# A four-layer graph network on one core: the gathers of layers 2 and 3 wait for two chunks at a time instead of eight

## What is computed

```python
# layer 2
K, Q, V = x_aug @ Wk, x_aug @ Wq, x_aug @ Wv            # 8 heads of 16
attn = einsum('ehd,ehd->eh', Q[dst], K[src]) * rel_scale[rel] / 4
attn_exp = exp(attn - max(attn))
out = segment_sum(attn_exp / (segment_sum(attn_exp)[dst] + 1e-16) * V[src])
# layer 3
scores = einsum('ehd,ehd->eh', q[src], k[tgt]) / 4 + edges @ We + be
scores = scores * cons[tgt] + mlp(distances)
weights = exp(scores - segment_max(scores)[tgt]) / segment_sum(...)[tgt]
agg = segment_sum(weights * v[tgt])
```

## Time and profile before

| | |
|---|---|
| median of three executions | 8839.98 us (8818.74 to 8856.99) |
| the profiled execution | 8825.96 us, its span 8824.2 us |
| busy over the span: PE, DVE, POOL, ACT | 65%, 56%, 54%, 13% |
| mean granted TensorE clock | 0.69 of full speed |
| gathers of layer 2: first, last start | 5723.2, 7302.6 us |
| gathers of layer 3: first, last start | 7425.1, 8709.4 us |

### The profile page before, as it was taken

One profiled execution on the slowest core, in us unless ns is written; L12 is line 12 of the kernel. 1 busy time (PEld: TensorE's weight loads), 2 busy tenths in 40 slices (PEclk: granted clock), 3 DMA queues, 4 the chain that ended last, 5 costly groups with the idle time before them and its releaser, 6 DMA issues. The chain is left out here.

```text
span 8824.2 us, 135351 instructions
## 1 busy us (share of the span) xinstructions
PE 5731.9 (65%) x29121; PEld 4795.7 (54%) x29122; DVE 4911.5 (56%) x17353; ACT 1162.1 (13%) x3262; POOL 4752.3 (54%) x4627
## 2 busy tenths in 40 slices
PE   6555555677767767777777999756666665333334
PEld 5555554566656656666664666456666664333333
DVE  6555554455555645555556888645555553444445
ACT  1111111111111101111112222100000002000001
POOL 2655665455555445555544777445554542666664
PEclk6555555777777878777778999866566666555556
DMA  5334334333333333333332444333333333333332
GB/s 155 95 93 96 96 94 105 116 96 93 95 94 93 75 89 97 92 96 93 97 77 45 60 63 60 84 83 89 90 91 87 90 87 52 74 75 75 75 77 48
DMA packets 919075, 759.30 MB, mean 86 GB/s; under 512 B 585447, under 2 KB 750451, under 8 KB 916947
## 3 DMA queue, kind: packets, MB, share of 16 engines
q0 software_dynamic: 233264, 421.09, 19.7%
q1 hardware_dynamic: 676780, 323.84, 15.2%
q10 hardware_dynamic: 8960, 13.52, 0.6%
HBM read 676.11 MB, written 80.55 MB: 86 GB/s over the span
## 5 line engine op out<-in xcount | busy, mean ns | idle before, releaser
L1180 POOL DMA_INDIRECT there<-table_wide,idx x1664 | 1596.4, 959 | 1382.6 <-DVE prod L1203 620.3
L1271 PE MATMUL ps<-here,hot_t 128*128 x3328 | 1228.1, 504 | 619.1 <-DVE there L1222 586.0
L2273 POOL DMA_INDIRECT there<-table_wide,idx x832 | 793.6, 954 | 888.6 <-DVE msg L2349 416.6
L1222 DVE TENSOR_TENSOR there<-there,ps 128x512 f32<-128x512 f32 x832 | 571.0, 686 | 1148.5 <-remote 579.9
L1271 PEld LDWEIGHTS ps<-here,hot_t 128*128 128x128 f32 x3328 | 735.1, 245 | 740.6 <-issue 653.8
L693 POOL DMA_INDIRECT rec<-out_recd,posd x806 | 819.1, 1016 | 568.9 <-issue 228.8
L2888 POOL DMA_INDIRECT there<-table_narrow,idx x832 | 791.2, 951 | 615.5 <-issue 252.4
L1279 PE MATMUL ps<-relu,hot_s 128*128 128x128 f32 x3328 | 885.5, 359 | 137.6 <-DVE hot_s L1211 111.1
L3048 PE MATMUL ps<-here,hot_t 128*128 x1664 | 426.5, 432 | 813.5 <-DVE prod L2969 403.1
L1279 PEld LDWEIGHTS ps<-relu,hot_s 128*128 128x128 f32 x3328 | 689.9, 239 | 328.3 <-issue 274.8
L3048 PEld LDWEIGHTS ps<-here,hot_t 128*128 128x128 f32 x1664 | 363.7, 312 | 876.0 <-issue 875.4
(11 more groups left out here) (508 smaller groups left out, 9850.2 us busy)
## 6 DMA issues: line engine op xcount, KB each, us to landing
locrows<-loc_row SPq DMA_DIRECT2D x416, 256.0 KB
krowd<-key_row SPq DMA_DIRECT2D x201, 256.0 KB
there<-table_wide,idx POOLq DMA_INDIRECT x2496
src_rows1a<-slot_src_row SPq DMA_DIRECT2D x52, 512.0 KB
lrowd<-lo_row SPq DMA_DIRECT2D x201, 128.0 KB
attr_raw<-in_edge_attr SPq DMA_DIRECT2D x201, 128.0 KB
there<-table_narrow,idx POOLq DMA_INDIRECT x832
rec<-out_recd,posd POOLq DMA_INDIRECT x806
```

What stands on the lines that cost most here:

```text
L1180: nc.gpsimd.indirect_dma_start(there[:, j, q, :], None, table, bass.IndirectOffsetOnAxis(idx[:, j, q:q + 1], 0)).then_inc(gathered[j][q], 16)
L1222: nc.vector.tensor_tensor(pair, pair, ps[:, WORK, :], ALU.add).then_inc(summed, 1)
L1271: last = nc.tensor.matmul(ps[:, WORK, (q % 2) * 2 * F:(q % 2 + 1) * 2 * F], hot_t[:, j % 2, q * P:(q + 1) * P], here[:, :, :].rearrange("p ...
L2273: nc.gpsimd.indirect_dma_start(there[:, j, q, :], None, table, bass.IndirectOffsetOnAxis(idx[:, j, q:q + 1], 0)).then_inc(gathered[j][q], 16)
```

## The change

POOL waits before every second gather, for the piece that frees the two chunks it is about to overwrite, instead of once before all eight for all four pieces; `admitted` is counted up four times as often. Nothing else changes.

```diff
 # hgt_pass, layer 2
                 for j in range(RING):
                     pool.wait_ge(indexed[j], i * 16 + 16)
-                    pool.wait_ge(placed, i * (RING * PIECES) + ((j + 1) * PIECES))
-                    pool.sem_inc(admitted, 1)
                     for q in range(U):
+                        if q % PIECE == 0:
+                            pool.wait_ge(placed, i * (RING * PIECES) + (j * PIECES + q // PIECE + 1))
+                            pool.sem_inc(admitted, 1)
                         nc.gpsimd.indirect_dma_start(there[:, j, q, :], None, table, ...)
 # edge_scores, layer 3
                 for j in range(RING):
                     pool.wait_ge(indexed, i * RING + (j + 1))
-                    pool.wait_ge(multiplied, i * (RING * PR) + (j * PR + PR))
-                    pool.sem_inc(admitted, 1)
                     for q in range(U):
+                        if q % 2 == 0:
+                            pool.wait_ge(multiplied, i * (RING * PR) + (j * PR + q // 2 + 1))
+                            pool.sem_inc(admitted, 1)
                         nc.gpsimd.indirect_dma_start(there[:, j, q, :], None, table, ...)
```

## The result

The changed kernel took 8869.2 us (median of 20 executions), the kernel before on the same chip 8827.4 us: a ratio of 1.0047 (1.0032 to 1.0062). A second comparison gave 1.0041 (1.0019 to 1.0063). So the change costs about 40 us, where a gain of 99 us had been forecast; 8869.2 us lies outside the stated range of 8690 to 8860. The profiled execution took 8864.5 us, its span is 8862.8 us.

What follows compares the result with a forecast made beforehand. No engine was full; layer 2's loop from `msg` through gather batch and first product bound it, 15.13 us a group. 98 x 1.01 = 99 us off the 8840 us median gave 8741, predicted 8742, range 8690 to 8860.

Steps and rivals of the forecast that it cites:

- The batch's start: Layer 2: the first gather waits for the first `msg`, not the fourth, so the batch begins 1.01 us earlier, still 0.78 us behind.
- What 1.01 us is worth: Layer 2's loop: the batch's progress lets the product go, so each round shortens by 1.01 us; 98 x 1.01 = 99 us.
- no change: Rival: layer 2's product release is tied to something DVE times, such as SyncE's loads; 8825 to 8840 us, chance 0.20.
- the 4.35 us: Layer 2: time from a first product to the end of the `msg` behind it, read from one round.
- The gathers as the cause: Layer 2: gathers being issued and landing hold the product; without them first products stand 7.62 us apart, half of 15.13.
- The added instructions at 0: Both layers: three more waits and three more `sem_inc` a group run while the gather before them works; cost 0.
- the 0.9 that I gave: Most the added waits and counts could cost if not covered: one more 0.30 us gap each, 0.9 us a group.
- Slower: Rival: layer 2's second product falls beside the batch and is held, 2.2 x 98 = 215 us, 9055 us; chance 0.13.
- The shared port: Rival: layer 2's first gather contends for SBUF with the last `msg` and second product; gain only 23 us, 8817; chance 0.08.

Runs made afterwards that it cites:

- experiment 4: Kernel before, layer 2's gather batch waiting also for the group's second product (ratio 0.9991), or for the one-hot matrix behind it (0.9989).
- experiment 5: Kernel before, layer 2's batch waiting also for the first product two groups on (0.9722), or the `hot_s` behind it (all gathers 0.9772; gathers 6 to 8 0.9761).
- experiment 6: Kernel before, layer 2 without SyncE's loop loads of `rel` (0.9979) or target rows (0.9964), or with four of eight gathers from the fifth group on (0.9495).
- experiment 8: Against the kernel before: layer 3 with seven more counts (1.0007) or the change's layer-3 part (1.0004), unchanged kernel then 6956.1 us; full change again (1.0041), l2_gate_first again (0.971).
- l2_more_waits: Kernel before, layer 2 with its old start plus three already met waits and three counts a group: 1.0051, layer 2 at 1631.2 us.
- l3_more_counts: Kernel before, layer 3 counting `admitted` up ahead of each of its eight gathers, seven more counts a group: 1.0007.
- l3_only_b: Kernel before with the change's waits in layer 3 alone, run once more on another occasion: 1.0004.
- l2_gate_first: Kernel before, layer 2's batch waiting also directly for the first product two groups on: 0.9722, 8595.8 us, rounds of 13.11 us.
- l2_late_start: Kernel before, layer 2's batch waiting also for the one-hot matrix behind the second product: 0.9989, layer 2 at 1611.3 us.

## Why the prediction was wrong

**The batch's start: right.** 0.78 us after the first `msg`, and 1.01 us earlier within the round; one burst of eight, 1.25 us apart.

**What 1.01 us is worth: the step that failed.** I wrote "I take 1.01, since the two batches of the earlier trace rows ... let the product go 9.3 and 8.6 us after their start", and treated that distance as fixed. It is not: it was 7.85, 9.5 and 11.5 us for three starts (experiment 4). The start 1 us earlier made the product come 2 us later behind it, so the step lost about 1 us where it was to win 1.01. Why an earlier start keeps TensorE's signal back longer stays open; how deep in the burst the half is due does not explain it by itself. The spread that I had noted under "no change" (8.6, 9.3, 10.0 on the mean: "no fixed distance") was the hint, though the 10.0 itself was misread: it took the 4.35 us of one round for the mean, and counted from the batches' starts the mean was 9.54.

**The gathers as the cause: right, though it was argued from a confounded row.** The earlier trace rows stand where SyncE's loads have ended too. Experiments 5 and 6 show that it is the gathers; experiment 8 shows that it takes something more, since on one occasion they kept nothing back.

**The added instructions at 0: wrong.** They leave the gathers 1.25 us apart, as forecast, but cost 0.52 us a round by the first product's lateness (l2_more_waits). That this lies within the 0.9 that I gave is luck: my bound was for longer gaps between gathers, and these did not grow. In the change about 0.1 of it shows, since the product is at the burst's end already. I looked at GpSimd's own time and not at the signals beside it. By what way a count keeps TensorE's signal back is not shown.

**The rivals.** No change had SyncE's loads as what lets the product go; without them the rounds stayed at 15.1 to 15.2 us (experiment 6), and in the change the product did not come when it had come before, but 1.14 us later behind the second one. Slower was on the right side with the wrong mechanism: the second product, 0.43 us into the burst, is never held, nor is it at 3.5 us (experiment 5). Its price of 215 us was for a wait of the second product that did not come. The shared port played no part that can be seen: the first gather took 1.04 for 0.95 us beside `msg`, 0.09 us.

The Trainium skill, Perfetto Trace Analysis, "Tensor Engine Instruction (MATMUL, LD_WEIGHTS)", says that a matmul's end in a profile is computed, and that the signal goes out only when PSUM has acknowledged the writes. The rows agree that the recorded end is no signal: 6581.35 and 6585.68. Whether the work, the acknowledgement or the signal is late, no run here shows.

## What to carry to other kernels

A wait whose end coincides with another transfer's landing need not keep its distance from the burst's start when the burst is moved: before moving a burst, ask which signals of other engines will fall beside it, and try more than one start. Placing a burst that is needed only rounds later (here behind the first product, 243 us faster) was worth more than starting it early, in the conditions of all occasions but one; how it does on that one was not measured. Waits and counts that cost their own engine nothing were not free for others.

## What the runs showed of the hardware

In all profiles but two (l3_more_counts and l3_only_b, of one occasion) TensorE's signals came late beside bursts of GpSimd's gathers. First halves that were due 2.7 to 7.2 us into a burst of eight came 3 to 7 us late on the mean; second halves due up to 3.5 us into it came at most 0.14 us late (l2_gate_first). In nearly all rounds the signal came no later than the last landing of the burst, and with two batches back to back it could be kept back through both, 15.55 us in the round shown (l2_late_start). DVE's signals were not late (0.01 us). Seven more counts a group made it worse (60 us in a layer). On one occasion the effect was absent and the same kernel took 6956 instead of 8840 us, a fifth less: more than any edit tried here gained.
